# A second weight-loading path on ScalarE for two projections, three buffers for the K and V weights, and earlier loads of the residual

## The chip, the cores and the metric

One Trainium2 chip, 8 cores, each running the same program on its own sequence of a batch of 8. The cores exchange nothing. The time is that of one execution on the device, in microseconds, on the slowest core.

## What is computed

A transformer layer on x of 2048 tokens x 2048 features: latent attention with 16 heads, residual, layer norm, a gated FFN, residual, layer norm. Cut to what matters:

```
q    = rmsnorm(x @ q_a_w.T) @ q_b_w.T          # 1536 -> 16 heads x (128 + 64)
ckv, k_pe = split(x @ kv_a_w.T)                # 512 latent + 64 rope columns
k_nope, v = split(rmsnorm(ckv) @ kv_b_w.T)     # per head: 128 + 128
q_pe, k_pe = rope(q_pe), rope(k_pe)
attn = softmax(causal([q_nope q_pe] @ [k_nope k_pe].T * 192**-0.5)) @ v
x1   = layernorm(x + attn @ o_w.T)
h    = silu(x1 @ gate_w.T * gate_s) * (x1 @ up_w.T * up_s)     # 5632 wide
out  = layernorm(x1 + h @ down_w.T * down_s)
```

All weights and x are fp32 in HBM; products run in bf16 with sums in fp32.

## The kernel before

The program is written as five instruction streams, one per engine. A helper `P.op` appends an instruction to the stream of its engine, `P.w` and `P.wf` append a wait for a semaphore; each engine executes its stream in the order in which it was written. `tMM` and `tTR` count finished products and transposes of TensorE (PE), `vE` and `vStat` operations of VectorE (DVE), `sAct` those of ScalarE (ACT), `cW` the casts of weights on DVE. `gate()` makes every engine wait for all of these at the borders of the phases.

The phases are: A1 (projections to the latents, all tokens; `rmsqa_fm`, `c_fm` and `kpe_lo` stay in SBUF), A2 (`q_group`: Q for all heads into `Q_all`), A3 (attention, one head after another, output in `OX`), A4 (output projection, residual, layer norm, transposes back to `OX`), and the FFN in four groups of 512 tokens.

Weights reach SBUF in two ways. `load_cast` cuts a tile into slices of 512 columns (256 KB): SyncE (SP) starts the DMA into one of two fp32 slots `stage` (L180) and DVE casts it to bf16 (L191); the slot is free after the cast. SP runs ahead, so the next two slices are always on their way. `mk_path` makes a path of its own with slots of 1024 columns; the FFN uses two of them, `lc_gp` (DMA from GpSimd's queue, cast on DVE) and `lc_sy` (DMA from SP's, cast on ACT), L221, L226 and L229. In such a path the wait for a free slot and the DMA are written to the stream of `eng`, the wait for the landing and the cast to that of `cast_eng`.

A2 has six groups (four of nope columns, then two of rope columns). Each takes 12 slices of 512 columns from a ring of 18 in `qbw_bf`; a slice of the ring is free when the group that used it has finished its last product. PE waits for all 12 casts, then computes 4 chunks x 4 pieces x 12 products (L548), and DVE evicts each piece (L558; for the rope groups L564 to L592, with one more product `pROT`, L576). The casts of the next group stand behind those evictions in DVE's stream. The rope tables `cosf`, `sinf` and `cRotT` (9 slices) are loaded by the same path ahead of group 0.

A3, per head: DVE casts the K weights into `kvw_bf`; PE computes `kfm` (L663, 4 pieces x 4 products; ACT evicts, L670); DVE waits for the last of these, casts the V weights into the same `kvw_bf`; PE computes `vtm` (L681, 16 chunks x 4 products, in two alternating PSUM banks; ACT evicts, L688). Then the 16 query chunks follow, software-pipelined: scores (L714 to L725), row maxima on DVE (L732), exp on ACT (L800), transposes with scaling (L767), `PTsb` (L774), product with V (L751), `OX` (L785). At head 8, GpSimd copies `kpe_lo` to its upper half by DMA and DVE clears the lower half (L648, L651), ahead of that head's casts.

A4: the 16 tiles of `ow_l`, 2048 columns each, are loaded by `load_cast` (64 slices). Then for each of 16 token tiles: GpSimd's queue loads `x` into one of two `xst4`, PE computes 64 products (L886; for token tile 0 it waits for each weight tile's cast), DVE adds the residual (L896), and the layer norm and transposes follow (L901 to L924, L861, L868).

## Time and profile before

| | us |
|---|---|
| median of 2 runs | 5623.71 |
| these runs | 5598.27 and 5649.15 |
| the profiled execution | 5649.49 |
| its span (core 2, the slowest) | 5647.9 |
| spans of the eight cores | 5570.3 to 5647.9 |

The profile is one execution on the slowest core. PE is busy for 3865.4 us of the span (68%), DVE for 1857.5 (33%), ACT for 1636.8 (29%), GpSimd for 317.8 (6%). HBM traffic is 119 GB/s over the span. Busy time is the sum of the instructions' durations on an engine; waits and DMA issues are not in it. An idle time is put down to whoever ended it last.

### The profile page before, as it was taken

The numbers are of one execution on the slowest core, as the hardware profiler recorded it, in microseconds if no ns is written. First come the engines' busy times: TensorE is split into PE (matmuls) and PEld (weight loads), VectorE is DVE, ScalarE is ACT, GpSimd is POOL, SyncE is SP. The second block draws the span as 40 slices with busy tenths as digits, with TensorE's granted clock in tenths as the row PEclk, the third lists the DMA queues.
The fourth block names the chain that finished last, engine by engine and source line by source line (L and its number), as shares of the span: only waits on it lengthen the run. The fifth ranks groups of instructions, "written<-read, shape, count | busy, mean of one in ns | idle before, by whom it ended". The sixth has DMA issues, their size and how long they took to land.

```text
span 5647.9 us, 67406 instructions; the slowest of 8 cores (5570.3 to 5647.9 us)
## 1 busy us (share of the span) xinstructions
PE 3865.4 (68%) x20400; PEld 1843.4 (33%) x20400; DVE 1857.5 (33%) x3822; ACT 1636.8 (29%) x3420; POOL 317.8 (6%) x581
## 2 busy tenths in 40 slices
PE   0466657466666666666256578895998599859886
PEld 0222323123333333333022233342434233423343
DVE  2233322443333333333232333323332333223323
ACT  0000000025656565665000023322332233223322
POOL 0000000000000000000000011110111111101111
PEclk9877778888788787887577789998999899979998
DMA  4200021100000000000410069876987698759975
GB/s 124 56 30 30 19 64 46 40 8 9 5 9 5 10 5 9 7 7 23 119 38 30 30 209 269 256 246 192 279 268 238 189 269 271 237 176 262 268 244 180
DMA packets 209874, 674.49 MB, mean 119 GB/s; under 512 B 30272, under 2 KB 30784, under 8 KB 205440
## 3 DMA queue, kind: packets, MB, share of 16 engines
q1 hardware_dynamic: 130608, 359.51, 20.6%
q0 software_dynamic: 78928, 310.68, 18.0%
q8 instruction: 187, 3.06, 0.2%
q14 instruction: 151, 1.24, 0.1%
HBM read 653.05 MB, written 16.78 MB: 119 GB/s over the span
## 4 chain that ended last, share of the span: by engine, by line
DMA 33%; PE 33%; DVE 12%; issue 11%; ACT 9%; DVEq 1%; SPq 0%; ACTq 0%; POOL 0%; POOLq 0%
DMA stg_gp<-up_l 20%; PE pD L1090 6%; DMA stg_gp<-down_c 5%; PE pPT L548 5%; PE pOP L886 4%; ACT Ebuf L800 4%; PE pQA L417 3%; PE pO L751 3%; ACT PTsb L774 2%; DVE ubf L229 2%; DMA stage<-ow_l 2%; PE pPT L767 2%; DVE stats L732 2%; PE pS L714 2%; DVE dbf L229 1%
## 5 line engine op out<-in xcount | busy, mean ns | idle before, releaser
L1019 PE MATMUL pU<-OX,ubf 128*128 128x512 bf16 x2816 | 650.6, 385 | 153.8 <-DVE ubf L229 152.7
L1010 PE MATMUL pG<-OX,gbf 128*128 128x512 bf16 x2816 | 643.7, 382 | 126.5 <-ACT gbf L226 126.5
L1090 PE MATMUL pD<-h_fm,dbf 128*128 128x512 bf16 x2816 | 642.2, 385 | 92.1 <-DVE dbf L229 87.7
L229 DVE CAST ubf<-stg_gp 128x1024 bf16<-128x1024 f32 x352 | 244.3, 694 | 902.0 <-DMA stg_gp<-up_l 882.1
L751 PE MATMUL pO<-PTsb,vtm 128*128 128x128 bf16 x2176 | 248.1, 246 | 314.6 <-ACT PTsb L774 311.2
L1019 PEld LDWEIGHTS pU<-OX,ubf 128*128 128x128 bf16 x2816 | 269.7, 99 | 526.4 <-issue 235.3
L1010 PEld LDWEIGHTS pG<-OX,gbf 128*128 128x128 bf16 x2816 | 277.1, 98 | 463.9 <-issue 136.8
L1090 PEld LDWEIGHTS pD<-h_fm,dbf 128*128 128x128 bf16 x2816 | 274.3, 99 | 438.5 <-issue 143.1
L1032 ACT ACTIVATE sig<-pG,gates_sb 128x512 bf16<-128x512 f32 x176 | 121.0, 687 | 908.7 <-DVE tmid L1037 753.4
L548 PE MATMUL pPT<-rmsqa_fm,qbw_bf 128*128 128x512 bf16 x1152 | 277.1, 402 | 137.9 <-DVE qbw_bf L191 137.8
L774 ACT CAST PTsb<-pPT 128x512 bf16<-128x512 f32 (+3 forms) x640 | 312.7, 525 | 199.1 <-PE pPT L767 198.1
L226 ACT CAST gbf<-stg_sy 128x1024 bf16<-128x1024 f32 x352 | 350.1, 1040 | 62.2 <-DMA stg_sy<-gate_l 62.0
L886 PE MATMUL pOP<-ow_bf,OX 128*128 128x512 bf16 x1024 | 280.5, 442 | 113.8 <-DVE ow_bf L191 111.2
L800 ACT ACTIVATE Ebuf<-pS,stats 128x512 bf16<-128x512 f32 (+3 forms) x512 | 314.6, 622 | 90.8 <-DVE stats L791 89.7
L226 ACT CAST dbf<-stg_sy 128x1024 bf16<-128x1024 f32 (+1 forms) x192 | 174.3, 971 | 548.7 <-PE pD L1090 548.7
L732 DVE TENSOR_REDUCE stats<-pS 128x1 f32<-128x512 f32 (+3 forms) x512 | 289.6, 599 | 122.4 <-PE pS L725 121.8
L229 DVE CAST dbf<-stg_gp 128x1024 bf16<-128x1024 f32 (+1 forms) x192 | 121.9, 648 | 559.3 <-DMA stg_gp<-down_c 293.5
L751 PEld LDWEIGHTS pO<-PTsb,vtm 128*128 128x128 bf16 x2176 | 155.1, 107 | 391.5 <-issue 389.7
L767 PE MATMUL pPT<-Dg,Ebuf 128*128 128x128 bf16 x2176 | 252.6, 254 | 26.8 <-DVE stats L732 23.5
L221 POOL DMA_DIRECT2D stg_gp<-up_l x352 | 194.6, 553 | 1265.9 <-DVE ubf L229 1174.8
L714 PE MATMUL pS<-kfm,Q_all 128*128 128x512 bf16 (+3 forms) x512 | 213.3, 417 | 71.3 <-ACT Ebuf L800 45.5
L417 PE MATMUL pQA<-qa_w_bf,x0fm_t 128*128 128x512 bf16 x768 | 237.0, 423 | 5.3 <-DVE c_fm L366 4.3
(132 smaller groups left out, 3727.6 us busy)
## 6 DMA issues: line engine op xcount, KB each, us to landing
stg_gp<-up_l POOLq DMA_DIRECT2D x352, 512.0 KB, 6.4
stg_sy<-gate_l SPq DMA_DIRECT2D x352, 512.0 KB, 6.5
stg_sy<-down_c SPq DMA_DIRECT2D x128, 512.0 KB, 5.4
stg_gp<-down_c POOLq DMA_DIRECT2D x128, 512.0 KB, 5.1
stg_sy<-down_c SPq DMA_DIRECT2D x64, 384.0 KB, 6.4
stg_gp<-down_c POOLq DMA_DIRECT2D x64, 384.0 KB, 4.5
stage<-x SPq DMA_DIRECT2D x64, 256.0 KB, 3.2
stage<-ow_l SPq DMA_DIRECT2D x64, 256.0 KB, 3.4
```

The costliest lines, as they stand in the source:

```text
L226: e.copy(d[:, a:a + cc], tiles[i][:, 0:cc]), inc=cP)
L229: e.tensor_copy(d[:, a:a + cc], tiles[i][:, 0:cc]), inc=cP)
L417: P.op("tensor", lambda e, i=i, d=d, j=j, st=st, sp=sp: e.matmul(pQA[:, j * 512:(j + 1) * 512], x0fm_t[i][:, d * 128:(d + 1) * 128], qa_w_ ...
L548: P.op("tensor", lambda e, pb=pb, sk=slots[k], k=k, cc=cc, piece=piece: e.matmul(pW[pb][:], qbw_bf[:, sk * 512 + cc * 128:sk * 512 + (cc + ...
L732: P.op("vector", lambda e, g=g, n=n, rt=rt, off=off, par=par: e.reduce_max(stats[:, par + g:par + g + 1], rt[:, off:off + n], axis=AX), in ...
L751: P.op("tensor", lambda e, kt=kt, bb=bb, sl=sl, nkt=nkt: e.matmul(pO[:, 0:128], vtm[:, kt * 128:(kt + 1) * 128], PTsb[sl][:, bb * 128:(bb ...
L774: P.op("scalar", lambda e, bn=bn, sl=sl: e.copy(PTsb[sl][:, 0:bn * 128], pPT[sl][:, 0:bn * 128]), inc=sAct)
L800: P.op("scalar", lambda e, ei=ei, g=g, n=n, rt=rt, off=off, par=par: e.activation(Ebuf[ei][:, g * 512:g * 512 + n], rt[:, off:off + n], AF ...
L886: P.op("tensor", lambda e, hv=hv, t=t, j=j, st=st, sp=sp: e.matmul(pOP[:, j * 512:(j + 1) * 512], OX[:, hv * S + t * 128:hv * S + (t + 1) ...
L1010: P.op("tensor", lambda e, wi=wi, d=d, gc0=gc0: e.matmul(pG[wi][:], gbf[wi][:, d * 128:(d + 1) * 128], OX[:, d * S + gc0:d * S + gc0 + 512 ...
L1019: P.op("tensor", lambda e, wi=wi, d=d, gc0=gc0: e.matmul(pU[wi][:], ubf[wi][:, d * 128:(d + 1) * 128], OX[:, d * S + gc0:d * S + gc0 + 512 ...
L1090: P.op("tensor", lambda e, di=di, hh=hh, jj=jj, ii=ii: e.matmul(pD[di][:], dbf[hh][:, jj * 128:(jj + 1) * 128], h_fm[:, ii * 512:(ii + 1) ...
```

## The change

Four edits:

- `mk_path` takes the width of its slots. In A2 a new path `lc_a2` (two slots of 512 columns, DMA and cast both on ACT) loads the odd slices of each group, `load_cast` the even ones. PE waits for both.
- In A3 the one buffer `kvw_bf` becomes three, `kvw3`. The weights of head h+1 are loaded and cast while head h is computed: K's after the K products of head h are written, V's after its V products. Those of head 0 come ahead of the loop.
- In A4 a new path `lc_a4` (two slots of 1024 columns, DMA and cast both on ACT) loads the odd weight tiles, `load_cast` the even ones.
- In A4 the `x` loads of token tiles 0 and 1 are written ahead of the weights, and that of tile t+2 behind the residual add of tile t, which frees the slot.

```diff
--- before.py
+++ after.py
@@ -203,8 +203,8 @@
                 c0 += cc
             return done
 
-        def mk_path(sb_fn, name, eng, cast_eng, nslots=2):
-            tiles = [sb_fn(f"stg_{name}{i}", [128, 1024], F32) for i in range(nslots)]
+        def mk_path(sb_fn, name, eng, cast_eng, nslots=2, slot_cols=1024):
+            tiles = [sb_fn(f"stg_{name}{i}", [128, slot_cols], F32) for i in range(nslots)]
             sems = [P.sem(f"d_{name}{i}") for i in range(nslots)]
             cP = P.sem(f"c_{name}")
             st = {"free": [None] * nslots, "i": 0}
@@ -213,7 +213,7 @@
                 done = None
                 c0 = 0
                 while c0 < cols:
-                    cc = min(1024, cols - c0)
+                    cc = min(slot_cols, cols - c0)
                     i = st["i"] % nslots
                     st["i"] += 1
                     P.wf(eng, st["free"][i])
@@ -513,6 +513,8 @@
 
                 pW = [ps2("pW0", [128, 512]), ps2("pW1", [128, 512])]
                 pROT = ps2("pROT", [128, 512])
+                lc_a2 = mk_path(sb2, "a2", "scalar", "scalar",
+                                nslots=2, slot_cols=512)
 
                 load_cast(cos_fm2_in, cosf, 0, S)
                 load_cast(sin_fm2_in, sinf, 0, S)
@@ -534,14 +536,20 @@
                     g = gidx[0]
                     gidx[0] += 1
                     slots = [(g * QLC + k) % 18 for k in range(QLC)]
+                    w_cp = None
                     for k in range(QLC):
-                        P.wf("vector", slot_free[slots[k]])
-                        load_cast(src[grp, k], qbw_bf, slots[k] * 512, 512)
+                        if k % 2 == 0:
+                            P.wf("vector", slot_free[slots[k]])
+                            load_cast(src[grp, k], qbw_bf, slots[k] * 512, 512)
+                        else:
+                            P.wf("scalar", slot_free[slots[k]])
+                            w_cp = lc_a2(src[grp, k], qbw_bf, slots[k] * 512, 512)
                     w_ready = cW.n
                     for cc, ch in enumerate(chunks):
                         for piece in range(NP):
                             pb = (cc * NP + piece) % 2
                             P.w("tensor", cW, w_ready)
+                            P.wf("tensor", w_cp)
                             P.w("tensor", vE, a1_done_v)
                             P.wf("tensor", pw_free[pb])
                             for k in range(QLC):
@@ -617,7 +625,7 @@
 
                 kfm = sb3("kfm", [128, S])
                 vtm = sb3("vtm", [128, S])
-                kvw_bf = sb3("kvw_bf", [128, LAT])
+                kvw3 = [sb3(f"kvw3_{i}", [128, LAT]) for i in range(3)]
                 Ebuf = [sb3(f"Ebuf{i}", [128, S]) for i in range(2)]
                 PTsb = [sb3(f"PTsb{i}", [128, 512]) for i in range(2)]
                 Dg = [sb3(f"Dg{i}", [128, 128]) for i in range(2)]
@@ -631,7 +639,6 @@
                 pW = pPT
 
                 kv_free = None
-                kvw_free = None
                 ppt_free = [None, None]
                 pw_free = ppt_free
                 e_free = [None, None]
@@ -640,6 +647,11 @@
                 rp = [0]
                 po_free = None
                 pts_free = [None, None]
+
+                kvw_ready = {}
+                kvw_ready[(0, 0)] = load_cast(kvbk_l[0], kvw3[0], 0, LAT)
+                kvw_ready[(0, 1)] = load_cast(kvbv_l[0], kvw3[1], 0, LAT)
+                vmm_prev = 0
 
                 kpe_shift_done = 0
                 for h in range(H):
@@ -650,19 +662,19 @@
                         P.w("vector", dSh, dSh.n)
                         P.op("vector", lambda e: e.memset(kpe_lo[0:64, :], 0.0), inc=vE)
                         kpe_shift_done = vE.n
-                    P.wf("vector", kvw_free)
-                    kw_ready = load_cast(kvbk_l[h], kvw_bf, 0, LAT)
+                    kw_sb = kvw3[(2 * h) % 3]
+                    vw_sb = kvw3[(2 * h + 1) % 3]
                     P.wf("tensor", kv_free)
-                    P.w("tensor", cW, kw_ready)
+                    P.w("tensor", cW, kvw_ready[(h, 0)])
                     P.w("tensor", vE, a1_done_v)
                     kpr = [None] * NP
                     for piece in range(NP):
                         pb = piece % 2
                         P.wf("tensor", pw_free[pb])
                         for l in range(LATC):
-                            P.op("tensor", lambda e, pb=pb, l=l, piece=piece: e.matmul(
+                            P.op("tensor", lambda e, pb=pb, l=l, piece=piece, w=kw_sb: e.matmul(
                                 pW[pb][:],
-                                kvw_bf[:, l * 128:(l + 1) * 128],
+                                w[:, l * 128:(l + 1) * 128],
                                 c_fm[:, l * S + piece * 512:l * S + (piece + 1) * 512],
                                 start=(l == 0), stop=(l == LATC - 1)),
                                 inc=(tMM if l == LATC - 1 else None))
@@ -671,17 +683,20 @@
                             kfm[:, piece * 512:(piece + 1) * 512], pW[pb][:]), inc=sAct)
                         pw_free[pb] = (sAct, sAct.n)
                         kpr[piece] = (sAct, sAct.n)
-                    P.w("vector", tMM, tMM.n)
-                    vw_ready = load_cast(kvbv_l[h], kvw_bf, 0, LAT)
-                    P.w("tensor", cW, vw_ready)
+                    kmm_done = tMM.n
+                    if h + 1 < H:
+                        P.w("vector", tMM, vmm_prev)
+                        kvw_ready[(h + 1, 0)] = load_cast(
+                            kvbk_l[h + 1], kvw3[(2 * h + 2) % 3], 0, LAT)
+                    P.w("tensor", cW, kvw_ready[(h, 1)])
                     for tch in range(TC):
                         pb = tch % 2
                         P.wf("tensor", pw_free[pb])
                         for l in range(LATC):
-                            P.op("tensor", lambda e, pb=pb, l=l, tch=tch: e.matmul(
+                            P.op("tensor", lambda e, pb=pb, l=l, tch=tch, w=vw_sb: e.matmul(
                                 pW[pb][:, 0:128],
                                 c_fm[:, l * S + tch * 128:l * S + (tch + 1) * 128],
-                                kvw_bf[:, l * 128:(l + 1) * 128],
+                                w[:, l * 128:(l + 1) * 128],
                                 start=(l == 0), stop=(l == LATC - 1)),
                                 inc=(tMM if l == LATC - 1 else None))
                         P.w("scalar", tMM, tMM.n)
@@ -689,7 +704,11 @@
                             vtm[:, tch * 128:(tch + 1) * 128], pW[pb][:, 0:128]), inc=sAct)
                         pw_free[pb] = (sAct, sAct.n)
                     kv_ready = sAct.n
-                    kvw_free = (tMM, tMM.n)
+                    vmm_prev = tMM.n
+                    if h + 1 < H:
+                        P.w("vector", tMM, kmm_done)
+                        kvw_ready[(h + 1, 1)] = load_cast(
+                            kvbv_l[h + 1], kvw3[(2 * h) % 3], 0, LAT)
 
                     kpe_t = kpe_lo
                     pch = 16 + h % 8
@@ -838,13 +857,24 @@
 
             pOP = ps4("pOP", [128, D])
             pTR4 = ps4("pTR4", [128, 512])
+            lc_a4 = mk_path(sb4, "a4", "scalar", "scalar",
+                            nslots=2, slot_cols=1024)
+
+            x4_free = [None, None]
+            x_ld4 = [None] * TC
+            for t in range(2):
+                P.op("gpsimd", lambda e, t=t, i=t % 2: e.dma_start(
+                    out=xst4[i][:], in_=x_hbm[t * 128:(t + 1) * 128, :]),
+                    inc=dGs[t % 2], k=16)
+                x_ld4[t] = dGs[t % 2].n
 
             ow_cast = []
             for d in range(DC):
-                ow_cast.append(load_cast(ow_l[d], ow_bf, d * D, D))
-            ow_ready = cW.n
-
-            x4_free = [None, None]
+                if d % 2 == 0:
+                    ow_cast.append((cW, load_cast(ow_l[d], ow_bf, d * D, D)))
+                else:
+                    ow_cast.append(lc_a4(ow_l[d], ow_bf, d * D, D))
+
             pop_free = None
             ptr4_free = None
             x1tm_free = [None, None]
@@ -872,15 +902,12 @@
 
             for t in range(TC):
                 i = t % 2
-                P.wf("gpsimd", x4_free[i])
-                P.op("gpsimd", lambda e, t=t, i=i: e.dma_start(
-                    out=xst4[i][:], in_=x_hbm[t * 128:(t + 1) * 128, :]), inc=dGs[i], k=16)
-                x_ld = dGs[i].n
+                x_ld = x_ld4[t]
                 P.w("tensor", sAct, heads_done_s)
                 P.wf("tensor", pop_free)
                 for hv in range(DC):
                     if t == 0:
-                        P.w("tensor", cW, ow_cast[hv])
+                        P.wf("tensor", ow_cast[hv])
                     st, sp = (hv == 0), (hv == DC - 1)
                     for j in range(4):
                         P.op("tensor", lambda e, hv=hv, t=t, j=j, st=st, sp=sp: e.matmul(
@@ -897,6 +924,12 @@
                 x2_done = vE.n
                 pop_free = (vE, x2_done)
                 x4_free[i] = (vE, x2_done)
+                if t + 2 < TC:
+                    P.wf("gpsimd", x4_free[i])
+                    P.op("gpsimd", lambda e, t2=t + 2, i=i: e.dma_start(
+                        out=xst4[i][:], in_=x_hbm[t2 * 128:(t2 + 1) * 128, :]),
+                        inc=dGs[i], k=16)
+                    x_ld4[t + 2] = dGs[i].n
                 P.w("vector", vE, x2_done)
                 P.op("vector", lambda e: e.reduce_sum(stats[:, 10:11], x2[:], axis=AX), inc=vStat)
                 P.w("vector", vStat, vStat.n)
```

## Rows read from the trace of the kernel before

**Rows 1.** Stretches: time, busy PE, PEld, DVE, ACT, POOL (count), clock, DMA share, GB/s

```profile
713.00:1200.00 487.00, 288.16 (x1184) 118.45 (x1184) 182.52 (x307) 0.00 (x0) 0.00 (x0) 0.83 0.14 44
1200.00:2671.00 1471.00, 983.04 (x7168) 549.54 (x7168) 534.72 (x1698) 881.63 (x2497) 0.64 (x1) 0.81 0.02 7
2671.00:2805.00 134.00, 27.98 (x60) 6.54 (x60) 25.95 (x61) 0.00 (x0) 1.10 (x2) 0.50 0.49 137
3275.00:5648.00 2373.00, 1951.33 (x8976) 884.88 (x8976) 765.34 (x1126) 675.23 (x776) 308.34 (x560) 0.94 0.78 241
```

**Rows 2.** The page: the chain that ended last, by engine

```profile
DMA 33%; PE 33%; DVE 12%; issue 11%; ACT 9%; DVEq 1%; SPq 0%; ACTq 0%; POOL 0%; POOLq 0%
```

**Rows 3.** Waits of PE by phase: us in total, times, longest

```profile
PE pPT L548 <- DVE qbw_bf L191: 137.8, 6, 39.4
PE pPT L663 <- DVE kvw_bf L191: 12.4, 2, 6.5
PE pOP L886 <- DVE ow_bf L191: 111.2, 16, 14.7
```

**Rows 4.** Timeline, a gap of A2: start, us, engine, line, op, idle before

```profile
796.68 0.75 DVE L558 TENSOR_SCALAR Q_all<-pPT,scl 128x512 bf16<-128x512 f32 x1 [1.84 <-PE pPT L548]
797.35 0.75 DVE L191 CAST qbw_bf<-stage 128x512 bf16<-128x512 f32 x2
800.61 0.43 DVE L191 CAST qbw_bf<-stage 128x512 bf16<-128x512 f32 x1 [2.51 <-DMA stage<-qbn_g]
...
815.12 0.43 DVE L191 CAST qbw_bf<-stage 128x512 bf16<-128x512 f32 x1 [0.97 <-DMA stage<-qbn_g]
...
815.91 43.10 PE L548 MATMUL pPT<-rmsqa_fm,qbw_bf 128*128 128x512 bf16 x192 [19.40 <-DVE qbw_bf L191]
```

**Rows 5.** DMA issues: KB, median us to landing; last row: `stg_gp` alone, extremes

```profile
stg_gp<-up_l POOLq DMA_DIRECT2D x352, 512.0 KB, 6.4
stage<-ow_l SPq DMA_DIRECT2D x64, 256.0 KB, 3.4
xst<-x POOLq DMA_DIRECT2D x16, 1024.0 KB, 5.2
stage<-qbn_g SPq DMA_DIRECT2D x48, 256.0 KB, 2.8
stg_gp<-down_c POOLq DMA_DIRECT2D x128, 512.0 KB, 5.1
DMA to landing us min/median/max: 3.4/6.0/17.9
```

**Rows 6.** ACT's casts of 1024 columns: ns min/median/max; then two in the timeline

```profile
L226 ACT CAST gbf<-stg_sy x352: 1032/1043/1047, 3291.4 to 5394.2; 128x1024 bf16<-128x1024 f32 x176
...
3303.14 1.98 ACT L226 CAST gbf<-stg_sy 128x1024 bf16<-128x1024 f32 x2
```

**Rows 7.** Timeline before head 8: the memset of DVE

```profile
1938.62 1.76 DVE L651 MEMSET kpe_lo<- 64x2048 bf16 x1 [11.34 <-DMA kpe_lo<-kpe_lo]
```

**Rows 8.** Timeline of head 7, between its K and V products

```profile
1848.81 0.59 ACT L670 CAST kfm<-pPT 128x512 bf16<-128x512 f32 x1 [0.28 <-PE pPT L663]
1848.89 0.43 DVE L191 CAST kvw_bf<-stage 128x512 bf16<-128x512 f32 x1 [11.51 <-PE pPT L663]
...
1849.58 0.61 PE L681 MATMUL pPT<-kvw_bf,c_fm 128*128 128x128 bf16 x8 [0.86 <-ACT kfm L670]
```

**Rows 9.** Timeline, loads of A4

```profile
2671.00 134.99 SPq L180 DMA_DIRECT2D stage<-ow_l  x64
...
2676.35 0.43 DVE L191 CAST ow_bf<-stage 128x512 bf16<-128x512 f32 x1 [0.97 <-DMA stage<-ow_l]
2684.04 0.94 DVE L191 CAST ow_bf<-stage 128x512 bf16<-128x512 f32 x2 [7.26 <-DMA stage<-ow_l]
...
2809.03 0.43 DVE L191 CAST ow_bf<-stage 128x512 bf16<-128x512 f32 x1 [0.19 <-DMA stage<-ow_l]
...
2809.60 1.86 PE L886 MATMUL pOP<-ow_bf,OX 128*128 128x512 bf16 x4 [6.17 <-DVE ow_bf L191]
```

## The prediction

> **What bounds the kernel now.** I read the profile in this order: the table by stretch, the chain that ended last, what TensorE (PE) waited for, the timeline of each kind of waiting place, and the landing times of the transfers. The stretches [rows 1] cut the span at the phases: Q projection (A2, 713 to 1200 us), attention (A3, to 2671), output projection (A4, to 3275) and FFN (2373 us). Over the whole span the chain is a third DMA and a third PE [rows 2], but most of that DMA share is the FFN's `up_l`, which the change does not touch; a share of the span says nothing about this edit. What counts is the time in which PE stands still for the weights that the change loads otherwise. That is one row per phase [rows 3]: 137.8 us in six waits in A2, 111.2 us in 16 waits in A4, and only 12.4 us in two waits in A3. At most 261 us can be had, 4.6% of the span.
>
> Why PE stands still is seen in a gap of A2 [rows 4]. The last eviction of a group starts at 796.68. DVE casts the two slices that were already in the two stage slots (797.35), then the next is cast at 800.61 and the twelfth at 815.12, and PE starts at 815.91. Each slot goes around in about 3.25 us (issue, landing, cast), two slices per round. It is a latency limit: the path moves 256 KB in 2.8 us from issue to landing [rows 5]. A4's load stretch (2671 to 2805) runs at 137 GB/s, while the FFN holds 241 GB/s over 2373 us [rows 1], and one 1 MB transfer of `x` lands in 5.2 us [rows 5]. So room is left for a third transfer in flight, and that is what the change adds: a path issued and cast by ScalarE (ACT), which is idle in A2 and in the load stretch (0.00 us busy in both [rows 1]).
>
> **The change, part by part.** The new path has two slots, yet issue, wait and cast stand in one in-order queue: the issue of a slice is behind the cast of the slice before it, so only one transfer of the path is ever in flight. A round costs landing time plus what ACT's queue needs between the landing and the next issue. No row shows a DMA issued by ACT. Its bounds: if the issue leaves while the cast still runs, some 0.3 us; if it waits for the cast's end, 0.3 us more than the cast, which is 1.04 us for 1024 columns [rows 6] and, by the eviction of 512 columns in 0.59 us [rows 8], about 0.6 us for 512 (my estimate). Two casts of 1.04 us, with a wait for another transfer between them, took 1.98 us together [rows 6], less than their sum. ACT's queue thus runs ahead of its engine, so I take the first bound.
>
> *A2.* The odd slices of groups 1 to 5 go to ACT. The ring has 18 slots, 12 per group, so slices 1, 3 and 5 are loaded while the group before computes. Slices 7, 9 and 11 wait for that group's last matmul, and then run one after another. With 2.8 us of landing, 0.3 us between, and 0.1 us for a third transfer in flight, a round is 3.2 us. Three rounds are 9.6 us, the last cast and the release of PE 0.9 us: a gap of 10.5 us. DVE's six slices (two ready, two more rounds of 3.25 us after 0.8 us for the eviction, then second slice, cast and release, 1.5 us) need about 8.8 us and are not last. The five gaps are now (137.8 - 39.4) / 5 = 19.7 us each [rows 3]: 5 x 9.2 = 46 us gained. Group 0 waits 39.4 us, behind the rope tables on the same path: six slices fewer for DVE are three rounds, 9.7 us, of which I give back 1.2 us to the extra traffic: 8.5 us. ACT's six slices (20 us) lie beside it. A2: 54.5 us. Bounds: a round of 2.85 us (no contention; gap 9.5) gives 51 + 9.7 = 61; a round of 4.2 us (the issue waits, landing 0.5 us slower; gap 13.6) gives 30 + 5 = 35.
>
> *A3.* The weights get three buffers, and both casts of head h+1 move into head h, ahead of its softmax, where DVE would sit idle for PE. The K cast was hidden anyway: PE waited for `kvw_bf` only in heads 0 and 8. Head 0 keeps its wait of 5.9 us (12.4 - 6.5). In head 8 the K cast was queued behind the shift DMA of `kpe_lo` and a memset of 1.76 us [rows 7]; now it is done long before, and the 6.5 us shrink to some 0.5: 6 us gained. The shift itself is needed only by the scores, 13 us later. For V, PE waited for the cast (1848.89, 0.43 us) and started at 1849.58 with two chunks back to back [rows 8]. Without the cast the first could start 0.8 us earlier, but the second waits for the last `kfm` eviction, which ends at 1848.81 + 0.59 = 1849.40, and can start about 1849.57 instead of 1849.80. The V loop alternates between two banks at 0.88 us per pair, so the later bank sets its end: 0.25 us per head, 4 us over 16. A3: 10 us. Bounds 6 (V gives nothing) and 16 (0.65 us per head). The K and V casts wait for matmuls long finished, so nothing queues behind them.
>
> *A4.* 64 slices of 512 columns on one path become 32 there, and 16 of 1024 columns on ACT. Now: issues from 2671.0, last slice cast at 2809.03, PE's last group at 2809.60 [rows 9], 138.6 us, some 5 us of it because the two `x` loads of 1 MB come first (the casts jump from 2676.35 to 2684.04, a round and a bit more than the usual 4.1 us). The DVE path halves: 16 rounds of 4.3 us + 5 = 74 us. The ACT chain is then last: 16 x (landing + 0.3). 512 KB land in 5.1 us beside other traffic (`down_c`) and in 6.4 us in the FFN's dense part (`up_l`); 256 KB of `ow_l` need 3.4 us [rows 5]. I take 5.0: 16 x 5.3 = 85 us, + 5 (the `x` loads) + 1.3 (last cast, release) = 91.3 us. Gain 47 us. Bounds: 16 x (6.4 + 1.04 + 0.3) + 6.3 = 130 us, gain 8; and a landing of 3.5 us (between 2.8 for 256 KB and 5.2 for 1 MB), where the DVE path's 72 us sets the end, gain 66. That `x` for tiles 0 and 1 is issued above the loop, and the others behind the residual add, changes no time: the POOL queue did nothing else, and issued them at the same moments.
>
> Extra waits of PE (one per group of 12 matmuls in A2, 96 in all) lie behind matmuls of 2.6 us. The half-speed matmuls at the start of each burst stay, since gaps of 10 us remain. The FFN keeps its time.
>
> A page speaks against all this. The Trainium skill, DMA: Bandwidth & Descriptors, section Issuing engines are not separate DMA queues, says that DMAs started from several engines share the same 16 DMA engines, so that this saves only the sequencer's issue time. By it only the issue time of the 52 moved transfers would be gained, at most 17 us, beside A3's 10. The trace bears out the shared engines, but shows them busy for only 49% of the load stretch of A4 and 14% of A2 [rows 1].
>
> **Sum.** 54.5 + 10 + 47 = 111.5 us. The profiled execution took 5649.5 us (span 5647.9, 1.6 us around it): 5538. It was the slower of the two before; the median, 5623.7, lies 25.8 us lower. 5623.7 - 111.5 = 5512 us, a ratio of 0.980.
>
> **Rivals.** *ACT's chain is slow* (0.2): issues wait for casts and landings stretch towards the FFN's. A2 gains 38, A4 15, A3 8: 61 us, 5563. For it: no row shows such an issue. Against: the two casts in 1.98 us.
> *Everything overlaps well* (0.2): rounds of 2.85 and 3.8 us, A4 limited by the DVE path: 61 + 12 + 66 = 139, 5485. For it: one `x` transfer's 5.2 us. Against: `ow_l` lands in 3.4 us even at 137 GB/s.
> *The engines, not the slots, are the limit* (0.06), the page's rule: each path slows as the other starts, gain at most 27 us, 5597.
> *Slower* (0.04): ACT's serial chain of A4 outlasts what it replaces. It decides from 138.6 - 6.3 = 132 us, 8.3 us per round. FFN landings went up to 17.9 us [rows 5]. At 15 us per round A4 would lose 108 us; at 9 us per round A2's gaps would be 28 us and group 0's wait 55, a loss of 56; less A3's 10 that is 5778. In a stretch at 137 GB/s I see no cause for such landings. Half of this chance stays under 2%.
>
> **Chances.** The forecast has 0.5. About 2% is what a measurement can tell from no change here, and that bound (112 us) lies on the forecast. So half of it (0.26) and all of the fast case but a little (0.2, with the spread of the runs 0.21) are faster by over 2%: 0.47. The rest of it, the slow chain, the bandwidth limit and half of the slower case are within 2%: 0.51. Slower: 0.02. The range goes from the fast case less half the spread of the two runs (25 us), 5462, to the slow chain with some of it, 5578.
>
> **What would show it.** Right: PE's wait for `qbw_bf` in A2 falls from 137.8 to about 83 us, with ACT casts as the releaser of groups 1 to 5; ACT-issued 256 KB spaced 3.2 us apart in the gaps, and 512 KB 5.3 us apart in A4; the last wait of A4 ends some 91 us after the first issue; head 8 starts without a wait for DVE; DMA in A4's loads near 200 GB/s. Wrong: ACT rounds longer by the cast (the issue waits for the engine), or stage rounds that lengthen from 3.25 and 4.1 us as much as the slices fall (bandwidth), or a FFN whose 2373 us move.

## The result, and the profile after

| | before | after |
|---|---|---|
| median (runs) | 5633.65 us (10) | 5601.98 us (11) |
| lowest | 5595.59 | 5525.47 |
| ratio after to before | | 0.9886, 95% [0.9831, 0.9941] |
| the profiled execution, its slowest core | 5649.49, core 2 | 5608.11, core 6 |

The change makes the kernel 1.1% faster. Measured a second time, as told below, it was 1.5% (0.9853 [0.9806, 0.9901]). Both intervals lie below 1, and the forecast was 2.0%. Some executions have a lower granted clock on some cores, whatever the kernel; ratios leave them out, and the phase times below are those of cores whose A2 ran at the full pace (2.59 us for a piece of 12 products).

The page of the kernel after: its span, the busy engines, the granted clock in 40 slices, and the chain by engine.

```profile
span 5606.6 us, 67082 instructions; the slowest of 8 cores (5563.3 to 5606.6 us)
...
PE 3990.0 (71%) x20050; PEld 1899.7 (34%) x20400; DVE 1828.9 (33%) x3754; ACT 1673.2 (30%) x3472; POOL 331.7 (6%) x581
...
PEclk9877778877878787878677699999888688889898
...
PE 49%; DMA 21%; DVE 10%; issue 10%; ACT 9%; DVEq 1%; SPq 0%; ACTq 0%; POOL 0%; POOLq 0%
```

PE shows more busy time than before (3990.0 against 3865.4 us) for the same products: its clock was lower. The stretches of core 6 (columns as in [rows 1]) tell where.

```profile
715.00:1178.00 463.00, 305.77 (x1160) 122.81 (x1184) 167.28 (x269) 22.23 (x36) 0.00 (x0) 0.83 0.16 46
1178.00:2657.00 1479.00, 980.67 (x7073) 557.68 (x7168) 534.62 (x1697) 880.01 (x2497) 0.64 (x1) 0.79 0.03 7
2657.00:2757.00 100.00, 27.74 (x62) 8.29 (x64) 13.71 (x33) 16.71 (x16) 1.09 (x2) 0.57 0.75 189
3227.00:5606.00 2379.00, 2067.52 (x8784) 925.59 (x8960) 761.12 (x1121) 674.37 (x776) 322.12 (x560) 0.88 0.75 241
```

This core computed its FFN at a clock of 0.88, where the core shown of before had 0.94 [rows 1]. A second execution of the same kernel had 0.94 there too, and serves for the comparison by phase. Here is the same core 2 in it: A2, A3, the loads of A4, the FFN.

```profile
703.00:1163.00 460.00, 305.55 (x1160) 122.90 (x1184) 167.31 (x270) 22.23 (x36) 0.00 (x0) 0.83 0.15 46
1163.00:2637.00 1474.00, 977.89 (x7073) 553.88 (x7168) 534.47 (x1697) 880.45 (x2497) 0.64 (x1) 0.80 0.02 7
2637.00:2739.00 102.00, 27.88 (x62) 8.21 (x64) 13.82 (x33) 16.71 (x16) 1.10 (x2) 0.54 0.73 185
3207.00:5540.00 2333.00, 1932.18 (x8784) 884.27 (x8960) 764.28 (x1121) 675.17 (x776) 319.55 (x560) 0.94 0.78 245
```

And what PE waited for in it (us in total, times, longest), to be read against [rows 3]:

```profile
PE pOP L913 <- DVE ow_bf L191: 74.1, 8, 21.5
PE pPT L556 <- DVE qbw_bf L191: 45.2, 2, 33.8
PE pPT L556 <- ACT qbw_bf L226: 44.1, 4, 11.3
PE pPT L675 <- DVE kvw L191: 5.8, 1, 5.8
```

Weights in A2: 137.8 us of waiting became 89.3. But A2 itself went from 487.0 only to 460.0 us: 48.5 us of waiting are gone, 27 us of time. Over all eight cores, medians of before (first profile) and of the second execution after:

| us | before | after | gained | forecast |
|---|---|---|---|---|
| A1 | 712 | 706 | 6 | 0 |
| A2 | 486.4 | 458.1 | 28 | 54.5 |
| A3 | 1473.9 | 1471.0 | 3 | 10 |
| A4 | 611.9 | 568.6 | 43 | 47 |
| FFN | 2303.4 | 2306.5 | -3 | 0 |

The 6 us of A1 stand in a phase that the change does not touch; no run explains them. Most of the loss against the forecast is A2's, and A2's two rope groups tell why. Their 32 pieces follow each other at 4.9 us when the 12 products run at full clock (2.75 us for 12), and at 6.6 us when most of them run at half clock (4.44 us). The 32 pieces have 31 intervals, and one of these is the gap between the two groups. In the kernel before, six to nine of the other 30 were long ones, on one core 14; now 14 to 19 are. Before, core 2, one slow piece and one fast:

```profile
1036.85 4.44 PE L548 MATMUL pPT<-rmsqa_fm,qbw_bf 128*128 128x512 bf16 x12
...
1043.11 0.38 PE L576 MATMUL pROT<-pe_raw,cRotT 128*128 128x512 bf16 x1 [1.82 <-DVE t L568]
1043.44 2.75 PE L548 MATMUL pPT<-rmsqa_fm,qbw_bf 128*128 128x512 bf16 x12
```

The stretches of these two bursts show the clock (third number from the right), 0.62 in the slow one and 1.00 in the fast one:

```profile
1036.85:1041.29 4.44, 4.43 (x13) 1.50 (x12) 1.87 (x3) 0.00 (x0) 0.00 (x0) 0.62 0.00 0
1043.44:1046.19 2.75, 2.75 (x13) 1.07 (x12) 1.87 (x3) 0.00 (x0) 0.00 (x0) 1.00 0.00 0
```

After, core 2 of the second execution:

```profile
999.83 0.38 PE L584 MATMUL pROT<-pe_raw,cRotT 128*128 128x512 bf16 x1 [1.83 <-DVE t L576]
1000.27 2.75 PE L556 MATMUL pPT<-rmsqa_fm,qbw_bf 128*128 128x512 bf16 x12
```

From the start of `pROT` to the start of the next 12 products it is 0.33 us before and 0.44 after. Ahead of those products PE now executes one wait more, for ACT's last cast, which was done long ago. The rope stretch (first to last eviction, less the gap between its two groups) took 158.5 us on core 2 before and 181.2 us after, 22.7 us more, where 32 times 0.11 us are 3.5. The rest is the clock: slow pieces are 18 on this core now, six before.

### The profile page after: what moved, and what is told of

It is laid out like the page before. It is cut to its first block, busy times and chain, and to the rows that moved or that the text cites. A ratio compares the mean times of both kernels' runs of the same rounds, so it can differ in the third digit from the quotient of the medians.

```text
span 5606.6 us, 67082 instructions; the slowest of 8 cores (5563.3 to 5606.6 us)
## 1 busy us (share of the span) xinstructions
PE 3990.0 (71%) x20050; PEld 1899.7 (34%) x20400; DVE 1828.9 (33%) x3754; ACT 1673.2 (30%) x3472; POOL 331.7 (6%) x581
## 4 chain that ended last, share of the span: by engine, by line
PE 49%; DMA 21%; DVE 10%; issue 10%; ACT 9%; DVEq 1%; SPq 0%; ACTq 0%; POOL 0%; POOLq 0%
DMA stg_gp<-up_l 10%; PE pD L1123 8%; PE pU L1052 7%; PE pG L1043 7%; PE pPT L556 5%; PE pOP L913 4%; DMA stg_gp<-down_c 4%; ACT Ebuf L819 4%; PE pQA L417 3%; PE pO L770 3%; ACT PTsb L793 2%; PE pPT L786 2%; DVE stats L751 2%; PE pS L733 2%; DMA stage<-ow_l 2%
## 5 line engine op out<-in xcount | busy, mean ns | idle before, releaser
L1043 PE MATMUL pG<-OX,gbf 128*128 128x512 bf16 x2760 | 699.2, 408 | 135.5 <-ACT gbf L226 131.9
L1052 PE MATMUL pU<-OX,ubf 128*128 128x512 bf16 x2756 | 695.5, 407 | 70.1 <-DVE ubf L229 65.3
L1123 PE MATMUL pD<-h_fm,dbf 128*128 128x512 bf16 x2756 | 659.3, 399 | 62.7 <-DVE dbf L229 54.4
L1043 PEld LDWEIGHTS pG<-OX,gbf 128*128 128x128 bf16 x2816 | 291.0, 103 | 514.2 <-issue 334.4
L1052 PEld LDWEIGHTS pU<-OX,ubf 128*128 128x128 bf16 x2816 | 286.2, 103 | 459.9 <-issue 291.9
L556 PE MATMUL pPT<-rmsqa_fm,qbw_bf 128*128 128x512 bf16 x1129 | 294.1, 422 | 99.5 <-ACT qbw_bf L226 79.5
L819 ACT ACTIVATE Ebuf<-pS,stats 128x512 bf16<-128x512 f32 (+3 forms) x512 | 314.7, 622 | 92.1 <-DVE stats L810 91.2
L221 POOL DMA_DIRECT2D stg_gp<-up_l x352 | 207.4, 589 | 1250.3 <-DVE ubf L229 1133.7
L733 PE MATMUL pS<-kfm,Q_all 128*128 128x512 bf16 (+3 forms) x464 | 198.2, 427 | 64.1 <-ACT Ebuf L819 44.0
```

The source lines that it names most:

```text
L556: P.op("tensor", lambda e, pb=pb, sk=slots[k], k=k, cc=cc, piece=piece: e.matmul(pW[pb][:], qbw_bf[:, sk * 512 + cc * 128:sk * 512 + (cc + ...
L819: P.op("scalar", lambda e, ei=ei, g=g, n=n, rt=rt, off=off, par=par: e.activation(Ebuf[ei][:, g * 512:g * 512 + n], rt[:, off:off + n], AF ...
L1043: P.op("tensor", lambda e, wi=wi, d=d, gc0=gc0: e.matmul(pG[wi][:], gbf[wi][:, d * 128:(d + 1) * 128], OX[:, d * S + gc0:d * S + gc0 + 512 ...
L1052: P.op("tensor", lambda e, wi=wi, d=d, gc0=gc0: e.matmul(pU[wi][:], ubf[wi][:, d * 128:(d + 1) * 128], OX[:, d * S + gc0:d * S + gc0 + 512 ...
L1123: P.op("tensor", lambda e, di=di, hh=hh, jj=jj, ii=ii: e.matmul(pD[di][:], dbf[hh][:, jj * 128:(jj + 1) * 128], h_fm[:, ii * 512:(ii + 1) ...
```

## The experiments

Ranges are over the cores with pieces of 2.59 us (for the change, first profile: cores 0, 1, 6 and 7). "Slow" counts the rope intervals over 5.8 us; the recorded expectations speak of 31 intervals, of which one, the gap between the two groups, is never counted here; "load" is from the first weight load of A4 to its first residual add.

| kernel | A2 | slow | A3 | A4 | load |
|---|---|---|---|---|---|
| before | 484 to 490, once 500 | 6 to 9, once 14 | 1470 to 1480 | 602 to 615 | 133 to 147 |
| the change | 458 to 464 | 16 to 18 | 1465 to 1478 | 560 to 570 | 91 to 100 |
| the change again | 455 to 462 | 14 to 19 | 1468 to 1474 | 563 to 574 | 92 to 104 |
| A2 alone | 452 to 467 | 12 to 21 | 1472 to 1485 | 601 to 614 | 130 to 133 |
| A3 alone | 482 to 490 | 5 to 9 | 1452 to 1459 | 601 to 614 | 130 to 145 |
| A4 alone | 476 to 487 | 3 to 8 | 1471 to 1485 | 557 to 570 | 87 to 99 |
| rope by the old path | 458 to 463 | 8 to 9 | 1453 to 1463 | 556 to 559 | 86 to 92 |
| two in flight | 458 to 477 | 14 to 24 | 1468 to 1477 | 570 to 585 | 86 to 106 |
| wait once | 432 to 443 | 2 to 9 | 1459 to 1470 | 557 to 574 | 87 to 105 |
| wait once, again | 429 to 446 | 2 to 7 | 1460 to 1466 | 557 to 570 | 87 to 102 |
| before, one wait more | 509 to 514 | 19 to 22 | 1477 to 1482 | 601 to 611 | 133 to 143 |
| wait once, late `x` | 431 to 440 | 2 to 5 | 1447 to 1470 | 557 to 570 | 87 to 100 |
| rope product deferred | 379 to 385 | 0 | 1466 to 1473 | 574 to 590 | 96 to 104 |
| all three | 377 to 382 | 0 | 1460 to 1467 | 563 to 574 | 94 to 105 |

**Part by part.** The kernel before with only the edits of A2:

> Only the edit of A2 is in; A3 and A4 are those of the kernel before. Theory 1 (the clock gives back): the five gaps of A2 shrink by 8 us each and the first wait by 6 us, 46 us in all, but A2 as a whole gets only some 27 us shorter (about 460 us against 486 on cores whose nope groups run at 2.59 us per piece), because in the two rope groups 16 to 18 of 31 pieces run at half speed instead of 7 to 9. Theory 2 (chance between executions): the count of slow rope pieces is anything between 5 and 18, and A2 is 440 to 460 us. A3 (1470 to 1480 us) and A4 (602 to 615) stay.

With only those of A3:

> Only the edit of A3 is in. My forecast: A3 gets 10 us shorter than 1470 to 1480 us, of it 6 us at head 8 and 0.25 us per head for V. Rival (the clock here too): head 8's 6 us are gained and the rest lies within the scatter of the eight cores (10 us), so 1465 to 1475. A2 (484 to 490 us, 7 to 9 slow rope pieces) and A4 (602 to 615) stay; if A2 shows 16 or more slow pieces here, the count has nothing to do with the edit of A2.

With only those of A4 (the path on ACT and the earlier `x` loads):

> Only the edit of A4 is in. A4 falls from 602 to 615 us to 560 to 574, its load stretch from 133 to 147 us to 91 to 103: both theories. A2 and A3 as before: 484 to 490 us with 7 to 9 slow rope pieces by theory 1, anything from 5 to 18 of them by theory 2.

Each part acts in its own phase, and no phase pays for another's. A2's edit by itself has the slow rope pieces (12 to 21), the other two leave them as they were. A3's gave 20 us against the two others, which have the old A3 (medians 1455 against 1475 and 1480 us), more than the 10 forecast and more than the whole change shows. The part on A3 below takes this up.

**The rope groups by the old path.** Their loads only go back to `load_cast`, and PE's wait for ACT goes with them:

```diff
-                        if k % 2 == 0:
+                        if k % 2 == 0 or is_pe:
                             P.wf("vector", slot_free[slots[k]])
```

> The changed kernel, but the two rope groups take all 12 slices by the old path. If slow rope pieces come from the denser work of PE ahead of them (the short gaps between groups), group 4 still follows three short gaps but has a long one (20 us) of its own, and the count stays above 12 of 31. If they come from something inside the rope groups (ACT's loads beside them, or the short gap right ahead), the count falls to the 7 to 9 of the kernel before, and A2 is 440 + 2 x 8 = 456 us with two long gaps back, no slower than the full change's 458 to 463.

The gap between the two rope groups is back at 27.5 us (19 with the new path) and yet A2 takes the same 458 to 463 us: 8 or 9 slow pieces instead of 14 to 19. In the rope groups the new path gained in the two gaps, ahead of each group, what it lost in the pieces. Whether the clock fell for the loads or for the wait this run can't tell.

**The change again, and the wait once.** The change itself, for a second profile and a ratio beside the others:

> The changed kernel once more. On cores whose nope groups run at 2.59 us per piece: A2 452 to 463 us with 12 to 21 of 31 slow rope pieces, A3 1453 to 1463 us (the edit of A3 alone measured 1452 to 1459, more than my 10 us of gain), A4 556 to 574 us. The sum of the phases then is 80 to 95 us below the kernel before, and the time 1.4 to 1.7% below it in executions with the full clock.

It measured a median of 5520.74 us (5505.52 to 5541.98), a ratio of 0.9853 [0.9806, 0.9901]. Then the loads left as they are and only PE's wait thinned out, from 96 to six:

```diff
-                            P.wf("tensor", w_cp)
+                            if cc == 0 and piece == 0:
+                                P.wf("tensor", w_cp)
```

> The changed kernel, but PE waits for ACT's casts only ahead of the first piece of a group, not ahead of each of its 16 pieces (15 waits fewer per group, all of them long satisfied). Theory W (the extra wait, some 0.05 us per piece, tips the rope groups to the lower clock): the rope pieces return from 4.98 to 4.92 us, the slow ones from 12 to 21 of 31 to 5 to 9, and A2 gets 15 to 20 us shorter: 440 to 446 us. Rival L (ACT's loads and casts beside the rope groups, or the shorter gap ahead of the second of them): the count stays at 12 to 21 and A2 at 452 to 463 us.

> The change with PE's wait for ACT's casts written only ahead of the first piece of each group of Q, as in the run before of this form, to have its ratio. If the wait written ahead of all 96 pieces costs the clock of the rope pieces, A2 takes 432 to 443 us again where the nope pieces run at 2.59 us (the change: 455 to 462), 2 to 9 of the 31 rope intervals are over 5.8 us (the change: 14 to 19), and the ratio to the kernel before is 0.980 to 0.983, near the forecast's 0.980. If the 21 us of the run before were an accident of one execution, A2 is back at 455 to 462 and the ratio is that of the change, 0.985 to 0.989.

A2 falls by another 21 and 23 us (medians 436.9 and 434.6 against 458.1), with 2 to 9 slow pieces, and `pROT` is again followed by the products after 0.34 us (1000.85, 1001.19). The second execution of this form gave a ratio of 0.9784 [0.9645, 0.9923]. So it was the wait, not the loads. The interval is too wide to tell this kernel from the change by total time; the phase times tell them apart.

**The opposite case.** The kernel before, with one satisfied wait of PE added ahead of each piece, on a semaphore that reached its value once, long before:

```diff
                             P.w("tensor", cW, w_ready)
+                            P.w("tensor", sAct, scl_done)
                             P.w("tensor", vE, a1_done_v)
```

> The kernel before, untouched but for one more wait of PE ahead of each piece of A2, on a count of ACT that was reached long before (no load, no cast, no path is added). Theory W (one more satisfied wait ahead of each piece costs 0.11 us between the rotation product and the next products, and tips the rope groups towards the lower clock): 12 to 21 of 31 slow rope pieces instead of 3 to 9, A2 15 to 20 us longer: 495 to 510 us. Rival (it needs the loads of ACT beside it): 3 to 9 slow pieces, A2 at most 3 us longer, 480 to 492.

Nothing else differs from the kernel before, and A2 takes 509 to 514 us: 24.5 us more in the median, with 19 to 22 slow pieces. They stand side by side, on core 4 nine in one group and eleven in the other. The stretch of the rope pieces, first eviction to last, on one core each of four kernels (columns as in [rows 1]; the third number from the right is the clock). Before, core 2:

```profile
1010.05:1195.83 185.78, 107.83 (x404) 40.01 (x403) 102.88 (x167) 0.00 (x0) 0.00 (x0) 0.88 0.04 15
```

The change, second execution, core 2:

```profile
959.52:1158.43 198.91, 127.16 (x396) 44.49 (x403) 100.32 (x161) 3.09 (x5) 0.00 (x0) 0.81 0.03 12
```

The wait once, core 2:

```profile
961.19:1136.00 174.81, 105.09 (x396) 39.63 (x403) 100.32 (x161) 3.09 (x5) 0.00 (x0) 0.91 0.04 14
```

Before with one wait more, core 4:

```profile
996.57:1208.44 211.87, 131.84 (x404) 45.31 (x403) 102.83 (x167) 0.00 (x0) 0.00 (x0) 0.79 0.05 13
```

DVE is busy for the same 100 to 103 us in all four. With the wait PE's products take 19 to 24 us more in busy time, at a granted clock of 0.81 and 0.79 against 0.88 and 0.91. The two runs show that the wait costs the clock. Why a delay of 0.1 us does so, and whether a delay of another kind would, no run shows.

**Two transfers in flight on ACT's path.** The issue of a slice is written ahead of the wait for the ring's slot and one slice further ahead, so that two are on their way, as on SP's path:

```diff
                             P.wf("scalar", slot_free[slots[k]])
-                            w_cp = lc_a2(src[grp, k], qbw_bf, slots[k] * 512, 512)
+                            w_cp = a2_cast(qbw_bf, slots[k] * 512)
+                            a2_more()
```

> The changed kernel, but ACT's path of A2 keeps two transfers in flight: the DMA of a slice goes out as soon as a stage slot is free, ahead of the wait for its place in the ring. My step in the prediction: the gap of A2 is set by ACT's three serial rounds; with two slices landed before the group ends only one round is left on ACT, and DVE's six slices set the gap: 8.8 to 9.5 us instead of 11.4, A2 9 to 12 us shorter. Rival (the transfers share a limit, so that DVE's rounds lengthen): the gap stays at 11 to 11.5 us, and DVE becomes its releaser.

PE's waits for `qbw_bf` stay at 91 to 96 us (the change: 86 to 93), and A2 is no shorter. The landing times say why (size, median us from issue to landing). The change, core 6:

```profile
stg_a<-ow_l ACTq DMA_DIRECT2D x16, 512.0 KB, 5.6
stage<-ow_l SPq DMA_DIRECT2D x32, 256.0 KB, 5.3
stg_a<-qbn_g ACTq DMA_DIRECT2D x24, 256.0 KB, 3.2
stage<-qbn_g SPq DMA_DIRECT2D x24, 256.0 KB, 3.4
```

Two in flight, core 0:

```profile
stg_a<-qbn_g ACTq DMA_DIRECT2D x24, 256.0 KB, 4.2
stage<-qbn_g SPq DMA_DIRECT2D x24, 256.0 KB, 4.0
```

On these cores four transfers at once land in 4.0 to 4.2 us, three in 3.2 to 3.4, two in 2.8 [rows 5]; the medians of all cores lie at 3.5 to 4.5, 3.0 to 3.5 and 2.7 to 2.8. In the gaps of groups 1 to 4 the core moves 139 to 146 GB/s before (core 2), 178 to 194 after (core 2, second execution) and 184 to 199 with two in flight (cores 0 and 2). The third transfer still brought much, the fourth next to nothing. The rule that was weighed as a rival, the same hardware for every issuer, so that another one gains little, describes the fourth transfer here, not the third. The Trainium skill states it (DMA: Bandwidth & Descriptors, Issuing engines are not separate DMA queues: DMAs of all engines run on the same 16 DMA engines, and another issuer saves only its issue time). No run gives SP's own path a third slot, so it is not shown that the third transfer needs another issuer; it may be the third slot alone.

**Late `x`.** The two 1 MB loads of A4 wait until weight tile 12 is cast (on top of the wait once):

```diff
             for t in range(2):
+                P.wf("gpsimd", ow_cast[12])
                 P.op("gpsimd", lambda e, t=t, i=t % 2: e.dma_start(
```

> The changed kernel with PE's wait for ACT only ahead of the first piece of a group, and the two x loads of A4 issued after weight tile 12 is cast instead of first. My term: they cost the load stretch 5 us, so it falls from 87 to 104 us to 82 to 99. Rival (in the changed kernel they cost two rounds, since the second casts came 10 us after the first): 10 us less, 77 to 94. A2 432 to 443 as with the single wait.

A gain is neither shown nor excluded. The load stretch has a median over the cores of 91 us (87 to 100) where the two kernels with early loads and the wait once have 97 and 100, about the 5 us of the term; but early loads reached 89 us in the median with the rope groups by the old path and 94 with A4 alone, and with late loads the last kernel below takes 104. The scatter is larger than the term.

**The rope product deferred.** `pROT` of a piece is issued behind the next piece's 12 products, with `pe_raw` and `t1` doubled. PE then no longer waits for DVE in each piece:

```diff
+                                if pend[0] is not None:
+                                    finish(*pend[0])
+                                pend[0] = (q, ch, piece, vE.n if pend[0] is None else pw_free[pb][1])
```

> The changed kernel, with the rotation product of a rope piece issued after the 12 products of the next piece (pe_raw and t1 in two buffers), so that PE does not stand still for DVE inside a piece. Theory (the clock follows PE's idle time inside the rope pieces): no slow pieces but the one at the start of each group, the interval is set by DVE's five operations, 3.1 to 3.4 us, and the two groups take 31 x 3.3 + 20 = 122 us instead of 191 to 200: A2 about 380 us. Rival (the clock stays low after the long gap ahead of each group, whatever PE does inside): pieces at 4.4 us and more, A2 420 us.

5526.81 us in the median (10 runs), the lowest 5425.53; ratio 0.9714 [0.9651, 0.9776]. A2 falls to 379 to 385 us with no slow piece left, although the wait for ACT still stands ahead of each. Core 2:

```profile
993.69 0.38 PE L540 MATMUL pROT<-pe_raw,cRotT 128*128 128x512 bf16 x1
994.17 2.75 PE L582 MATMUL pPT<-rmsqa_fm,qbw_bf 128*128 128x512 bf16 x12
996.95 0.38 PE L540 MATMUL pROT<-pe_raw,cRotT 128*128 128x512 bf16 x1
```

One piece every 3.26 us, less than the 4.4 us that a burst at half clock alone would take. Ahead of `pROT` PE waits for DVE only three times, 6.0 us in all on this core, where it was 31 times and 56.4 us in the change (second execution, core 2). The last run takes this, the wait once and the late `x` together:

> Both of these and the rotation product deferred by a piece: A2 380 us (the deferral alone measured 379 to 385 at full clock), A4 5 to 10 us below the change, the rest as the change. In executions at full clock 5620 - 85 - 78 - 7 = 5450 us; a ratio to the kernel before of 0.965 to 0.97, unless the lower clock in the FFN, as seen with the deferral alone, takes a part of it back.

Its median is 5534.02 us (8 runs), its lowest run 5415.86 us, 10 us below the lowest of the kernel with the deferral alone; there is no ratio for it. A2 is 377 to 382 us, so beside the deferral the wait once is worth some 4 us (medians 382.8 and 378.8).

## Why the prediction was right, and where it was not

**The shape was right.** The gain is the stretches in which PE stands still for weights, and a third transfer in flight shortens them. The forecast, 5512 us or a ratio of 0.980, promised too much. By the two ratios the kernel stands at 5560 and 5541 us against the 5623.7 us of before, both within the range. The shortfall is 48 and 29 us; by phase A2 accounts for 26 us of it, A3 for 7 and A4 for 4, and A1's unforecast 6 us make up for a part. That the time lay in the range is no proof of the terms: one of them, below, was missing.

**A2's gaps, 5 x 9.2 us: nearly right.** The issue leaves while the cast runs, the bound that was chosen, as a gap of core 0 after shows:

```profile
790.04 0.33 ACTq L221 DMA_DIRECT2D stg_a<-qbn_g  x1
...
792.81 0.62 ACT L226 CAST qbw_bf<-stg_a 128x512 bf16<-128x512 f32 x1 [46.30 <-DMA stg_a<-qbn_g]
...
796.71 0.62 ACT L226 CAST qbw_bf<-stg_a 128x512 bf16<-128x512 f32 x1 [3.28 <-DMA stg_a<-qbn_g]
796.83 0.33 ACTq L221 DMA_DIRECT2D stg_a<-qbn_g  x1
...
799.02 0.43 DVE L191 CAST qbw_bf<-stage 128x512 bf16<-128x512 f32 x1 [0.19 <-DMA stage<-qbn_g]
800.39 0.62 ACT L226 CAST qbw_bf<-stg_a 128x512 bf16<-128x512 f32 x1 [3.07 <-DMA stg_a<-qbn_g]
...
801.37 1.87 PE L556 MATMUL pPT<-rmsqa_fm,qbw_bf 128*128 128x512 bf16 x4 [11.47 <-ACT qbw_bf L226]
```

The issue starts 0.12 us after the cast's start. The first slice of this gap lands in 2.7 us, the other two rounds are 3.9 and 3.7 us, not 3.2: what is not landing is 0.2 us (0.3 was allowed), but the two landings took 3.7 and 3.5 us instead of 2.9. The median over all of ACT's slices is 3.2 us. ACT's cast is the releaser of four of the five gaps (second execution, core 2; the waits above). The gaps are (89.3 - 33.8) / 5 = 11.1 us on core 2, not 10.5; group 0 waits 33.8 us, not 30.9. In all 48.5 us of waiting gone, 54.5 forecast.

**A2's rope pieces, costed at nothing: the step that failed.** "Extra waits of PE lie behind matmuls of 2.6 us" holds for the nope groups, whose pieces kept their 2.59 us. In the rope groups PE is idle for 1.8 us in each piece, ahead of `pROT`, and nothing hides what follows. The trace of before had the row (1043.44 after 1043.11, with [1.82 <-DVE t] ahead), and it had the slow pieces, six of 30 on that core; I asked only about the start of a burst after a gap. The 0.11 us themselves are 3.5 us; the more frequent half clock makes it 20. This is shown by taking the wait away (-21 and -23 us) and by adding one to the kernel before (+24.5 us).

**A3, 10 us: both parts came, the total is 3 to 20.** Head 8 is as forecast: its casts, at 1822.10 and 1836.61 on core 6 of the first profile, are done long before its K products start at 1923.43; those behind the memset, at 1928.43 and 1929.03, are head 9's. PE's only wait for `kvw` is head 0's 6.1 us. From the first K product of head 7 to that of head 8 it was 97.4 us in the median of the cores before and is 91.2 in the second execution, 6 us less for the 6 forecast. V gave what was forecast too. In head 7 of the second execution, core 2:

```profile
1818.05 0.38 PE L696 MATMUL pPT<-kvw,c_fm 128*128 128x128 bf16 x4
1818.18 0.59 ACT L682 CAST kfm<-pPT 128x512 bf16<-128x512 f32 x1 [0.28 <-PE pPT L675]
...
1818.91 0.61 PE L696 MATMUL pPT<-kvw,c_fm 128*128 128x128 bf16 x8 [0.48 <-ACT kfm L682]
...
1825.58 0.27 ACT L703 CAST vtm<-pPT 128x128 bf16<-128x128 f32 x1 [0.40 <-PE pPT L696]
```

Before, the end of the V products of head 7 (its start is in [rows 8]):

```profile
1856.25 0.49 ACT L688 CAST vtm<-pPT 128x128 bf16<-128x128 f32 x2 [0.40 <-PE pPT L681]
```

The first chunk now starts alone and early, the second waits for the last `kfm` eviction, and from there the chunks run in pairs with one left over. From the end of the last `kfm` eviction to the end of the last `vtm` eviction it is 1825.85 - 1818.77 = 7.08 us; it was 1856.74 - 1849.40 = 7.34. These are the medians of the heads on every core but for 0.01 us: 0.26 us per head for 0.25 forecast, 4 us over 16.

So 10 us are there, and the rest, from -7 to +10 us, goes with the clock of the phase (0.81 to 0.83 where A3 took about 1455 us, 0.79 to 0.81 where it took 1464 to 1480). A part of it can be placed: from a head's first K product to the end of its last `kfm` eviction it takes 4.2 to 4.4 us in the fast heads, and mostly 5.7 to 6.8 in the others. In the median core ten of 16 heads were slow before (87.4 us in all, mean of the cores), 11 in the second execution after (92.5), and only seven with A3's edit alone (84.1). On core 2 before, the K products of head 7 had a clock of 1.00 and took 3.73 us, those of head 8 0.62 and 5.75 us. Why one kernel has more such heads than another with the same instructions there is open. The kernels with A3's edit and few slow rope pieces tend to be the faster ones in A3 too (1459 to 1470, 1460 to 1466, 1453 to 1463); no run explains it.

**A4, 47 us: 43.** Both paths are at work in the load stretch, here core 6 after:

```profile
2656.55 0.36 ACTq L221 DMA_DIRECT2D stg_a<-ow_l  x1
...
2662.24 1.04 ACT L226 CAST ow_bf<-stg_a 128x1024 bf16<-128x1024 f32 x1 [5.87 <-DMA stg_a<-ow_l]
...
2671.25 1.04 ACT L226 CAST ow_bf<-stg_a 128x1024 bf16<-128x1024 f32 x1 [7.97 <-DMA stg_a<-ow_l]
2671.32 0.34 ACTq L221 DMA_DIRECT2D stg_a<-ow_l  x1
...
2751.34 1.04 ACT L226 CAST ow_bf<-stg_a 128x1024 bf16<-128x1024 f32 x1 [4.97 <-DMA stg_a<-ow_l]
...
2752.64 0.43 DVE L191 CAST ow_bf<-stage 128x512 bf16<-128x512 f32 x1 [0.20 <-DMA stage<-ow_l]
2753.21 3.57 PE L913 MATMUL pOP<-ow_bf,OX 128*128 128x512 bf16 x8 [6.62 <-DVE ow_bf L191]
```

PE's last group starts 96.7 us after the first issue (87.6 us on core 0), forecast 91.3. The second ACT cast comes 9.0 us after the first, where the later rounds are 5.7 in the mean: the `x` loads cost about 3 us there (on core 0, 10.1 us beside rounds of 4.9: 5 us, as forecast). Whether late `x` loads bring them back stayed open. One sub-step was wrong: DVE's path was to be done after 74 us and ACT's to be last. Both end together, 1.3 us apart, and DVE is the releaser of all eight waits. SP's 256 KB land in 5.3 us, 3.4 before [rows 5]: the paths slow each other, until both take 96 us on this core. The stretch moves 189 GB/s with the DMA engines busy for 75% ([rows 1]: 137 GB/s and 49%), as forecast near 200.

**The rivals.** None came: ACT's issues do not wait for casts; the full overlap (rounds of 2.85 us) is excluded by the landing times; the rule of the shared engines came in only at the fourth transfer.

## What to carry to other kernels

A wait that is always satisfied is free only where it stands behind work that the engine is still doing. Look for the place where it stands between the end of an idle time and the next burst of products, and write it once per group of data, not per use. And where a trace shows bursts that run now and then at half clock, do not price a new instruction ahead of them by its own length alone: each further burst that fell to half clock cost 1.7 us here, the instruction 0.11.

A second loading path pays where the first is limited by its slots: read it from the round (issue, landing, cast) and from the share of busy DMA engines, and expect the landings of the old path to stretch as the new one starts.

## What the runs showed of the hardware

- A wait of PE that had been satisfied long ago cost 0.11 us (0.33 to 0.44 us from `pROT` to the next products). Written ahead of all 96 pieces, it turned about 10 further ones of the rope groups to half clock, and taking it away or adding it moved A2 by 21 to 25 us.
- A DMA issued by ACT leaves 0.01 to 0.13 us after the start of the cast that is written ahead of it where it waits for nothing else (cast 2671.25, issue 2671.32) and keeps the queue for 0.33 us.
- 256 KB land in 2.7 to 2.8, 3.0 to 3.5 and 3.5 to 4.5 us with two, three and four transfers in flight (medians by core in A2: before, the change, two in flight); 512 KB beside two of 256 KB in 4.7 to 5.7 us (A4, the change).
- One core moved 139 to 146 GB/s with two transfers of 256 KB in flight, 178 to 194 with three and 184 to 199 with four (the gaps of A2).
